# Feed-forward of a decoder layer: on VectorE the third h value moves ahead of the two roundings, and the next tile's first h value ahead of the second maximum

## The chip, the cores and the metric

The kernel runs on one core of one Trainium2 chip. The metric is the device time of one execution in microseconds (us). The engines are named as the profile names them: PE is TensorE's matmuls, PEld its weight loads, DVE is VectorE, ACT is ScalarE, POOL is GpSimd, SP is SyncE.

## The reference, cut to what matters

A decoder layer over 4 x 512 = 2048 tokens of 512 values: windowed attention, a routed expert layer, and a quantized feed-forward. The change lies in the feed-forward alone:

```python
def bit_linear(x, w):           # both sides rounded: x to 8 bits per token, w to -1, 0, 1
    return einsum('bsh,oh->bso', activation_quant(x), weight_quant(w))
def activation_quant(x):
    s = 127 / clip(max(abs(x), axis=-1), 1e-5)
    return clip(round(x * s), -128, 127) / s
h = silu(bit_linear(x, w_gate)) * bit_linear(x, w_up)     # 512 -> 2048
h = ln_weight * (h * rsqrt(mean(h * h) + 1e-6))
y = bit_linear(h, w_down)                                  # 2048 -> 512
x = x + y                                                  # x was layer-normed first
```

So each token needs the mean square and the largest weighted absolute value over all 2048 of its h values before the first of them can be rounded.

## The kernel before, in words

There is no scheduler: each engine has a program written out by hand, and runs its instructions in that order. Semaphores between the engines are waited for by the instruction in front, so everything behind it on that engine waits too.

The feed-forward goes over 16 tiles of 128 tokens (`TILES`), and each tile's 2048 h values are made in four chunks c = 0 to 3 of 512 columns (`FC`, `CHK`). A name such as h2 below means chunk 2 of h. Around one chunk stand these steps:

- PE, `gate_up(t, c)`: four matmuls for the gate sums and four for the up sums, in two pairs of PSUM buffers in turn. It may write pair c % 2 again once the h value two chunks back exists. The profile calls the four buffers `e_xT_ps`, `up_ps`, `e_z_ps` and `e_aT_ps`, since the expert phase used the same space.
- ACT, `gate_of(t, c)`: silu of the gate sums into `f_gate` (L1746).
- DVE, `hidden(t, c)`: h = up sums x scale x gate (L1784), one input from PSUM and one from SBUF. It counts up `h_ready`.
- POOL, `weighted(t, c)`: h times the norm's weight, into `hw`, which the profile calls `xg_own` (L1695), 128x512 in SBUF from two SBUF inputs.

Once per tile, one tile late (for t - 1 while tile t's chunks are made), come: on DVE `top_of(t-1, 0)` and `top_of(t-1, 1)`, the largest absolute value of each half of `hw` (L1800, `hw_max`); on ACT `squares` (L1754), sums of squares by halves; on DVE `sum_squares(t-1)` (L1805, L1807); on POOL `rms_of(t-1)`, a power of -1/2 (L1691, `h_rms`); on DVE `scale_h(t-1)` (L1813 to L1822), five operations on one column that end in `h_mul`; on DVE `quantize_h(t-1)`, the two roundings (L1831, `hq_big`), each 128x1024 floats from SBUF to SBUF, called hq0 and hq1 below; on ACT `pack(t-1, 0)` and `pack(t-1, 1)` (L1739, `hq`), which narrow the codes, in order after `gate_of(t, 2)` and ahead of `gate_of(t, 3)`. SP transposes the halves by DMA, and PE multiplies them into the output two tiles late (`down`, L1906), a quarter behind each `gate_up`. DVE adds the output to x (`y_of`, L1836), and POOL scatters it and fetches a later tile (`store`, `gather`).

Between these stand the front steps for the layer norm and rounding of the x of later tiles: `mean_of`, `top_of_x` (L1191), `scale_x`, `quantize_x` (L1206, `xq_big`, 128x512 from SBUF to SBUF), `stats_of` and `variance_of` on DVE.

POOL's order within tile t is: `rms_of(t-1)`, `weighted(t, 0)`, `weighted(t, 1)`, `weighted(t, 2)`, `rstd_of`, `weighted(t, 3)`, `gu_scale_of`, `store`, `gather`. The four products are called w0 to w3 below.

Of the kernel before, what the change touches and what calls it, by code (L numbers as in the profile page):

```python
# [1579 lines left out]
def ffn_phase(nc, ctx, io, x2, y, sh, front):  # L1580
# [59 lines left out]
    def inside(t):  # L1640
        return 0 <= t < TILES

    def flat(tile, i):
        return tile[:, i].rearrange("p c n -> p (c n)")
# [17 lines left out]
    def sums_of(t):  # L1662
        return gate_ps[0][:] if t == TILES - 1 else up_ps[0][:] if t == TILES - 2 else y_ps[:]
# [115 lines left out]
    def vector_program(dve):  # L1779
        def hidden(t, c):  # L1780
            i = t % 2
            dve.wait_ge(gate_ready, t * FC + c + 1)
            dve.wait_ge(up_summed, t * FC + c + 1)
            nc.vector.scalar_tensor_tensor(h[:, i, c, :], up_ps[c % 2][:], gu_scale[:, i, 1:2], gate[:, c % 2, :],  # L1784
                                           ALU.mult, ALU.mult).then_inc(h_ready, 1)

        def weighted_last():
            t, c = TILES - 1, FC - 1
            dve.wait_ge(h_ready, TILES * FC)
            nc.vector.tensor_tensor(hw[:, t % 2, c, :], h[:, t % 2, c, :], ln_w[:, c * CHK:c * CHK + CHK], ALU.mult)\  # L1790
                .then_inc(hw_last_ready, 1)

        def top_of(t, n):
            i = t % 2
            if (t, n) == (TILES - 1, HALVES - 1):
                dve.wait_ge(hw_ready, TILES * FC - 1)
                dve.wait_ge(hw_last_ready, 1)
            else:
                dve.wait_ge(hw_ready, t * FC + 2 * n + 2)
            nc.vector.tensor_reduce(hw_max[:, i, n:n + 1], flat(hw, i)[:, n * HALF:n * HALF + HALF], AX.X, ALU.max,  # L1800
                                    apply_absolute_value=True).then_inc(hw_max_ready, 1)

        def sum_squares(t):
            dve.wait_ge(sq_ready, (t + 1) * HALVES)
            nc.vector.tensor_reduce(h_ss[:], h_sq[:, t % 2, :], AX.X, ALU.add).then_inc(ss_ready, 1)  # L1805
            dve.wait_ge(ss_ready, t + 1)
            nc.vector.tensor_scalar(h_var[:], h_ss[:], 1.0 / F, RMS_EPS, ALU.mult, ALU.add).then_inc(h_var_ready, 1)  # L1807

        def scale_h(t):
            i = t % 2  # L1810
            at = t * HQ_STEPS
            dve.wait_ge(hw_max_ready, (t + 1) * HALVES)
            nc.vector.tensor_reduce(h_top[:], hw_max[:, i, :], AX.X, ALU.max).then_inc(hq_step, 1)  # L1813
            dve.wait_ge(hq_step, at + 1)
            dve.wait_ge(rms_ready, t + 1)
            nc.vector.tensor_scalar(h_max[:], h_top[:], h_rms[:], Q_EPS, ALU.mult, ALU.max).then_inc(hq_step, 1)
            dve.wait_ge(hq_step, at + 2)
            nc.vector.reciprocal(h_inv[:], h_max[:]).then_inc(hq_step, 1)
            nc.vector.tensor_scalar(y_scale[:, t % (LATE_DOWN + 2):t % (LATE_DOWN + 2) + 1], h_max[:], w_mean[:, 2:3], 1.0 / QMAX, ALU.mult, ALU.mult)\
                .then_inc(hq_step, 1)  # L1820
            dve.wait_ge(hq_step, at + 4)
            nc.vector.tensor_scalar(h_mul[:], h_inv[:], h_rms[:], QMAX, ALU.mult, ALU.mult).then_inc(hq_step, 1)  # L1822

        def quantize_h(t):
            i = t % 2
            dve.wait_ge(hq_step, (t + 1) * HQ_STEPS)
            for n in range(HALVES):
                cols = slice(n * HALF, n * HALF + HALF)
                if inside(t - 1):
                    dve.wait_ge(hq_packed, (t - 1) * HALVES + n + 1)  # L1830
                nc.vector.tensor_scalar(hq_big[:, cols], flat(hw, i)[:, cols], h_mul[:], CODE, ALU.mult, ALU.add)\  # L1831
                    .then_inc(hq_ready, 1)

        def y_of(t):
            dve.wait_ge(y_summed, t + 1)
            nc.vector.scalar_tensor_tensor(xt[t], sums_of(t), y_scale[:, t % (LATE_DOWN + 2):t % (LATE_DOWN + 2) + 1], xt[t],  # L1836
                                           ALU.mult, ALU.add).then_inc(y_ready, 1)

        for t in range(TILES):
            if inside(t + 2):  # L1840
                front.mean_of(dve, t + 2)
            if inside(t - 1):
                top_of(t - 1, 0)
            if inside(t - LATE_DOWN - 1):
                y_of(t - LATE_DOWN - 1)
            if inside(t - 1):
                top_of(t - 1, 1)
            hidden(t, 0)
            if t == 0:
                dve.wait_ge(front.product_ready, ROUTED_TILES)  # L1850
                nc.vector.tensor_tensor(xg[last_expert], y_ps[:], xg[last_expert], ALU.add).then_inc(front.x2_ready, 1)
            if inside(t - 1):
                sum_squares(t - 1)
            if inside(t + 2):
                front.top_of_x(dve, t + 2)
            hidden(t, 1)
            if inside(t + 2):
                front.scale_x(dve, t + 2)
            if inside(t - 1):
                scale_h(t - 1)  # L1860
                quantize_h(t - 1)
            hidden(t, 2)
            if inside(t + 2):
                front.quantize_x(dve, t + 2)
            if inside(t + 3):
                front.stats_of(dve, t + 3)
                front.variance_of(dve, t + 3)
            if t == TILES - 1:
                top_of(t, 0)
            hidden(t, 3)  # L1870
        last = TILES - 1
        weighted_last()
        top_of(last, 1)
        sum_squares(last)
        scale_h(last)
        quantize_h(last)
        y_of(last - LATE_DOWN)
        for t in range(TILES - LATE_DOWN, TILES):
            y_of(t)

    def tensor_program(pe):
# [43 lines left out]
        for g in range(FC):  # L1925
            if g + 1 < FC:
                transpose_h(last, g + 1)
            down(last, g)

    return sync_program, gpsimd_program, scalar_program, vector_program, tensor_program  # L1930


# [93 lines left out]
```

## Time and profile before

| | us |
|---|---|
| median of 3 executions (788.45 to 791.21) | 789.06 |
| the profiled execution, its own time | 788.65 |
| its span | 786.6 |
| DVE busy in the span | 592.7 (75%) |
| PE busy in the span | 734.1 (93%) |
| POOL busy in the span | 331.8 (42%) |
| granted clock of PE, mean of the span | 0.989 |

The span is the time from the first to the last instruction of the profiled execution; the 2.05 us beside it are outside the program. Shares of the whole span mix three phases: attention up to about 455 us, the experts up to about 590 us, the feed-forward behind that. Times in rows of the trace count from the span's start.

### The profile page before, as it was taken

To read this page: it belongs to the slowest core of one execution; us is meant where nothing else is said; L and a number is where in the kernel's file an instruction comes from. 1 tells how busy PE (TensorE), PEld (TensorE's weight loads), DVE (VectorE), ACT (ScalarE), POOL (GpSimd) and SP (SyncE) were. 2 spreads that over 40 slices of the span, in tenths; PEclk is the share of its full clock that TensorE was granted. 3 is DMA by queue.
4 is the path that set the end of the run, shared out by engine and by line. 5 is a ranking of instruction groups with operands and counts; after the bars stand their busy time and mean duration, and the time that the engine had idled before them with its cause. 6 is when DMAs were issued, how large, how long until landed. Compare 5 with 4: busy or idle time off the path is not lost.

```text
span 786.6 us, 14189 instructions
## 1 busy us (share of the span) xinstructions
PE 734.1 (93%) x5167; PEld 509.8 (65%) x5184; DVE 592.7 (75%) x1099; ACT 473.0 (60%) x1028; POOL 331.8 (42%) x329
## 2 busy tenths in 40 slices
PE   5988999999999999999987989999998999999993
PEld 4765777777777776777764678888874444444441
DVE  6886866886667866766666547888888999999992
ACT  4565666766676665766666314444456777667761
POOL 2011205213242134254554444445546577778661
PEclk9999999999999999999999999999999999999998
DMA  9300012304030321314301366555341133334241
GB/s 311 119 1 27 28 47 89 105 31 162 29 108 28 108 93 70 108 38 152 129 34 55 54 216 261 186 200 196 118 134 30 41 95 80 98 91 107 70 92 40
DMA packets 55474, 78.33 MB, mean 100 GB/s; under 512 B 36335, under 2 KB 38383, under 8 KB 53680
## 3 DMA queue, kind: packets, MB, share of 16 engines
q1 hardware_dynamic: 46336, 51.99, 20.8%
q0 software_dynamic: 8784, 24.93, 9.7%
q8 instruction: 43, 0.70, 0.4%
q10 hardware_dynamic: 288, 0.52, 0.2%
q14 instruction: 23, 0.19, 0.1%
HBM read 56.92 MB, written 17.59 MB: 95 GB/s over the span
## 4 chain that ended last, share of the span: by engine, by line
PE 61%; DVE 21%; issue 7%; ACT 5%; POOL 3%; DMA 1%; another core or an unknown queue 0%; SPq 0%; ACTq 0%; POOLq 0%; DVEq 0%
PE side_ps L889 17%; PE pT_ps L976 9%; PE e_z_ps L1528 7%; PE y_ps L1528 7%; PE s_ps L948 5%; PE pv_ps L998 5%; DVE h L1784 4%; DVE hw_max L1800 4%; DVE hq_big L1831 3%; ACT hq L1739 2%; DVE neg_max L724 2%; PE s_ps L956 2%; PE pT_ps L889 1%; DVE probs L745 1%; ACT probs L548 1%
## 5 line engine op out<-in xcount | busy, mean ns | idle before, releaser
L548 ACT ACTIVATE probs<-s_ps,neg_max 128x512 f32<-128x512 f32 (+2 forms) x256 | 152.3, 610 | 18.6 <-DVE neg_max L724 17.1
L724 DVE TENSOR_REDUCE neg_max<-s_ps 128x2 f32<-128x1024 f32 (+2 forms) x128 | 124.5, 1014 | 36.2 <-PE s_ps L956 35.1
L976 PE MATMUL pT_ps<-ident,probs 128*128 128x128 f32 x832 | 115.7, 281 | 8.7 <-DVE probs L745 8.0
L560 ACT ACTIVATE probs<-pT_ps 128x512 f32<-128x512 f32 x96 | 57.4, 598 | 97.0 <-PE pT_ps L976 96.2
L976 PEld LDWEIGHTS pT_ps<-ident,probs 128*128 128x128 f32 x832 | 94.3, 144 | 23.9 <-DVE probs L745 10.6
L745 DVE COPY probs<-pT_ps 128x512 f32<-128x512 f32 x112 | 76.7, 685 | 38.9 <-PE pT_ps L976 35.9
L1695 POOL TENSOR_TENSOR xg_own<-h,ln_w_sb 128x512 f32<-128x512 f32 x63 | 82.8, 1324 | 33.2 <-DVE h L1784 33.1
L889 PE MATMUL side_ps<-w_hi 128*128 128x512 f32 x172 | 71.0, 413 | 0.0
L412 POOL TENSOR_TENSOR aT_hi<-norm,one_col 128x512 fp32r<-128x512 f32 x15 | 15.6, 1042 | 124.6 <-DVE norm L736 86.3
L889 PE MATMUL side_ps<-w_hi,w_lo 128*128 128x512 f32 x172 | 67.4, 392 | 0.0
L889 PE MATMUL side_ps<-w_lo,w_hi 128*128 128x512 f32 x172 | 67.0, 390 | 0.0
L1906 PE MATMUL y_ps<-w_tern,hqT 128*128 128x512 bf16 x210 | 54.5, 379 | 0.7
L998 PE MATMUL pv_ps<-probs,v_sb 128*32 128x256 f32 (+1 forms) x896 | 52.4, 368 | 1.9 <-DVE probs L745 0.9
L404 POOL TENSOR_TENSOR norm<-rinv,one_col 128x512 f32<-128x512 f32 x16 | 16.7, 1041 | 86.8 <-DVE rinv L731 86.8
L548 ACT ACTIVATION_READ_ACCUMULATOR probs<-s_ps,neg_max 128x1 f32 x256 | 52.9, 207 | 0.0
L1739 ACT ACTIVATE hq<-hq_big,minus_offset 128x1024 bf16<-128x1024 f16 x30 | 33.0, 1142 | 30.4 <-DVE hq_big L1831 30.4
L1657 PE MATMUL e_xT_ps<-w_tern,xqT_home 128*128 128x512 bf16 x126 | 32.7, 380 | 7.1 <-DVE h L1784 6.2
L1800 DVE TENSOR_REDUCE hw_max<-xg_own 128x1 f32<-128x1024 f32 x32 | 38.7, 1209 | 0.3
L998 PEld LDWEIGHTS pv_ps<-probs,v_sb 128*32 128x32 f32 x896 | 25.0, 109 | 19.6 <-issue 6.7
L889 PEld LDWEIGHTS side_ps<-w_hi,w_lo 128*128 128x128 f32 x172 | 32.3, 188 | 7.4
L1906 PEld LDWEIGHTS y_ps<-w_tern,hqT 128*128 128x128 bf16 x224 | 21.4, 98 | 23.3
L889 PEld LDWEIGHTS side_ps<-w_hi 128*128 128x128 f32 x172 | 32.4, 188 | 5.8 <-DVE k_lo L648 0.5
(290 smaller groups left out, 1782.8 us busy)
## 6 DMA issues: line engine op xcount, KB each, us to landing
w_piece<-w_ffn SPq DMA_DIRECT2D x24, 512.0 KB
w_stage<-w_ffn SPq DMA_DIRECT2D x12, 1024.0 KB
xres<-x POOLq DMA_DIRECT2D x4, 1024.0 KB, 6.4
xn<-x SPq DMA_DIRECT2D x3, 1024.0 KB
x<-xres POOLq DMA_DIRECT2D x3, 1024.0 KB, 4.8
xn<-c SPq DMA_DIRECT2D x2, 1024.0 KB, 5.0
v_next<-c SPq DMA_DIRECT2D x2, 1024.0 KB, 7.3
xn<-x SPq DMA_DIRECT2D x4, 256.0 KB, 3.7
```

Source lines behind the costliest of these rows:

```text
L548: nc.scalar.activation(weights[qt][:, h, at:at + width(qt)], s_ps[:, h, 0:width(qt)], ACT.Exp, bias=neg_max[:, qt % 2, h:h + 1], accum_out ...
L560: nc.scalar.activation(out, turned_p, ACT.Identity).then_inc(slot_copied[0], 1)
L724: nc.vector.tensor_reduce(neg_max[:, qt % 2, 2 * s:2 * s + 2], s_ps[:, 2 * s:2 * s + 2, 0:width(qt)], AX.X, ALU.max, negate=True).then_inc ...
L745: nc.vector.tensor_copy(weights[qt][:, :, a:z], pT_ps[:, 1, :].rearrange("p (h n) -> p h n", h=GH))\
L889: last = nc.tensor.matmul(out, lt, r, start=(first and n == 0), stop=(final and n == len(terms) - 1))
L976: last = nc.tensor.transpose(pT_ps[:, k % 2, h * P:h * P + P], weights[qt][:, h, a:z], ident[:])
L998: last = nc.tensor.matmul(pv_ps[HD * h:HD * h + HD, to], v_sb[:, slot, f:f + HD], p, start=first, stop=final, tile_position=(0, HD * h))
L1528: last = nc.tensor.matmul(out, lt[:, k, :], r[:, at, :], start=(n == 0), stop=(n == 3 * DK - 1))
L1695: nc.gpsimd.tensor_tensor(hw[:, t % 2, c, :], h[:, t % 2, c, :], ln_w[:, c * CHK:c * CHK + CHK], ALU.mult)\
L1739: nc.scalar.activation(hq[:, cols], hq_code[:, cols], ACT.Identity, bias=minus_offset[:]).then_inc(hq_packed, 1)
L1800: nc.vector.tensor_reduce(hw_max[:, i, n:n + 1], flat(hw, i)[:, n * HALF:n * HALF + HALF], AX.X, ALU.max, apply_absolute_value=True).then_ ...
L1906: last = nc.tensor.matmul(sums_of(t), hqT[:, t % 2, k, :], down_w[:, k, :], start=(k == 0), stop=(k == FK - 1))
```

## The change

Within one tile of the DVE program, two steps change places with a neighbour. The instructions, their shapes, their buffers and their waits stay as they are, and so do the programs of the other engines.

```diff
             if inside(t - LATE_DOWN - 1):
                 y_of(t - LATE_DOWN - 1)
-            if inside(t - 1):
-                top_of(t - 1, 1)
             hidden(t, 0)
...
             if inside(t - 1):
                 sum_squares(t - 1)
+                top_of(t - 1, 1)
             if inside(t + 2):
                 front.top_of_x(dve, t + 2)
             hidden(t, 1)
...
             if inside(t - 1):
                 scale_h(t - 1)
+            hidden(t, 2)
+            if inside(t - 1):
                 quantize_h(t - 1)
-            hidden(t, 2)
             if inside(t + 2):
                 front.quantize_x(dve, t + 2)
```

The first place is on DVE at the start of a tile in the middle of the feed-forward (`h<-up_ps` is h0 here, `hw_max` the maxima, `xn<-y_ps` the output's addition). Before:

```order
L1800 TENSOR_REDUCE hw_max<-xg_own 128x1
L1836 SCALAR_TENSOR_TENSOR xn<-y_ps,y_scale,xn 128x512
L1800 TENSOR_REDUCE hw_max<-xg_own 128x1
L1784 SCALAR_TENSOR_TENSOR h<-up_ps,gu_scale,f_gate 128x512
L1805 TENSOR_REDUCE h_ss<-h_sq 128x1
L1807 TENSOR_SCALAR h_var<-h_ss 128x1
L1191 TENSOR_REDUCE x_max<-f_xn 128x1
```

And of the change, the same stretch:

```order
L1836 SCALAR_TENSOR_TENSOR xn<-y_ps,y_scale,xn 128x512
L1784 SCALAR_TENSOR_TENSOR h<-up_ps,gu_scale,f_gate 128x512
L1805 TENSOR_REDUCE h_ss<-h_sq 128x1
L1807 TENSOR_SCALAR h_var<-h_ss 128x1
L1800 TENSOR_REDUCE hw_max<-xg_own 128x1
L1191 TENSOR_REDUCE x_max<-f_xn 128x1
```

The second maximum has moved behind h0, `h_ss` and `h_var`, and stands in front of `x_max`.

The second place is later in the same tile on DVE, around the two roundings (`h<-up_ps` is h2 here, `hq_big` x2 are hq0 and hq1). Before:

```order
L1819 TENSOR_SCALAR y_scale<-h_max,w_mean 128x1
L1822 TENSOR_SCALAR h_mul<-h_inv,h_rms 128x1
L1831 TENSOR_SCALAR hq_big<-xg_own,h_mul 128x1024 x2
L1784 SCALAR_TENSOR_TENSOR h<-up_ps,gu_scale,f_gate 128x512
L1206 TENSOR_SCALAR xq_big<-f_xn,x_inv 128x512
```

And of the change:

```order
L1819 TENSOR_SCALAR y_scale<-h_max,w_mean 128x1
L1822 TENSOR_SCALAR h_mul<-h_inv,h_rms 128x1
L1784 SCALAR_TENSOR_TENSOR h<-up_ps,gu_scale,f_gate 128x512
L1831 TENSOR_SCALAR hq_big<-xg_own,h_mul 128x1024 x2
L1206 TENSOR_SCALAR xq_big<-f_xn,x_inv 128x512
```

h2 now stands between `h_mul` and the roundings.

## Rows read from the trace of the kernel before

**Rows 1.** The profile's page: the chain that ended last, by engine.

```profile
PE 61%; DVE 21%; issue 7%; ACT 5%; POOL 3%; DMA 1%; another core or an unknown queue 0%; SPq 0%; ACTq 0%; POOLq 0%; DVEq 0%
```

**Rows 2.** Busy time by engine in a stretch: tiles 0 to 13 of the feed-forward.

```profile
core 0: us, PE busy (x) PEld busy (x) DVE busy (x) ACT busy (x) POOL busy (x), PEclk, DMA share, GB/s
592.60:743.20 150.60, 143.41 (x675) 62.98 (x686) 142.88 (x318) 107.67 (x162) 107.01 (x113) 1.00 0.29 75
```

**Rows 3.** DVE in order of time: h3 of tiles 0, 13 and 14.

```profile
598.26 0.75 DVE L1784 SCALAR_TENSOR_TENSOR h<-e_aT_ps,gu_scale,f_gate 128x512 f32<-128x512 f32 x1
...
743.17 0.75 DVE L1784 SCALAR_TENSOR_TENSOR h<-e_aT_ps,gu_scale,f_gate 128x512 f32<-128x512 f32 x1 [1.11 <-ACT f_gate L1746]
...
753.67 0.75 DVE L1784 SCALAR_TENSOR_TENSOR h<-e_aT_ps,gu_scale,f_gate 128x512 f32<-128x512 f32 x1 [1.13 <-ACT f_gate L1746]
```

**Rows 4.** DVE in order of time, from h3 of tile 8 to h3 of tile 9.

```profile
687.05 0.75 DVE L1784 SCALAR_TENSOR_TENSOR h<-e_aT_ps,gu_scale,f_gate 128x512 f32<-128x512 f32 x1
687.72 0.20 DVE L1186 TENSOR_SCALAR mean_rstd<-f_bn_mv,f_rstd 128x1 f32<-128x1 f32 x1
687.84 1.21 DVE L1800 TENSOR_REDUCE hw_max<-xg_own 128x1 f32<-128x1024 f32 x1
...
689.63 1.21 DVE L1800 TENSOR_REDUCE hw_max<-xg_own 128x1 f32<-128x1024 f32 x1
690.75 0.74 DVE L1784 SCALAR_TENSOR_TENSOR h<-up_ps,gu_scale,f_gate 128x512 f32<-128x512 f32 x1
...
691.59 0.15 DVE L1807 TENSOR_SCALAR h_var<-h_ss 128x1 f32<-128x1 f32 x1
...
692.26 0.74 DVE L1784 SCALAR_TENSOR_TENSOR h<-e_aT_ps,gu_scale,f_gate 128x512 f32<-128x512 f32 x1
...
693.90 0.21 DVE L1822 TENSOR_SCALAR h_mul<-h_inv,h_rms 128x1 f32<-128x1 f32 x1
694.15 1.30 DVE L1831 TENSOR_SCALAR hq_big<-xg_own,h_mul 128x1024 f32<-128x1024 f32 x1
695.37 0.74 DVE L1831 TENSOR_SCALAR hq_big<-xg_own,h_mul 128x1024 f32<-128x1024 f32 x1
696.03 0.73 DVE L1784 SCALAR_TENSOR_TENSOR h<-up_ps,gu_scale,f_gate 128x512 f32<-128x512 f32 x1
696.69 0.47 DVE L1206 TENSOR_SCALAR xq_big<-f_xn,x_inv 128x512 f32<-128x512 f32 x1
...
698.28 0.75 DVE L1784 SCALAR_TENSOR_TENSOR h<-e_aT_ps,gu_scale,f_gate 128x512 f32<-128x512 f32 x1
```

**Rows 5.** POOL in the same tile: w3 of tile 8, then w0, w1, w2.

```profile
687.88 1.27 POOL L1695 TENSOR_TENSOR xg_own<-h,ln_w_sb 128x512 f32<-128x512 f32 x1 [0.29 <-DVE h L1784]
...
692.40 2.49 POOL L1695 TENSOR_TENSOR xg_own<-h,ln_w_sb 128x512 f32<-128x512 f32 x2
...
696.85 1.45 POOL L1695 TENSOR_TENSOR xg_own<-h,ln_w_sb 128x512 f32<-128x512 f32 x1 [1.96 <-DVE h L1784]
```

**Rows 6.** ACT in the same tile: the gate of h0, then the two packs.

```profile
689.21 0.67 ACT L1746 ACTIVATE f_gate<-e_xT_ps,gu_scale 128x512 f32<-128x512 f32 x1
...
695.48 1.15 ACT L1739 ACTIVATE hq<-hq_big,minus_offset 128x1024 bf16<-128x1024 f16 x1 [2.17 <-DVE hq_big L1831]
...
696.54 1.13 ACT L1739 ACTIVATE hq<-hq_big,minus_offset 128x1024 bf16<-128x1024 f16 x1
```

**Rows 7.** Tile 14: DVE's roundings hq0, hq1 and POOL's w0, w1.

```profile
749.31 0.88 DVE L1831 TENSOR_SCALAR hq_big<-xg_own,h_mul 128x1024 f32<-128x1024 f32 x1
...
750.11 1.76 DVE L1831 TENSOR_SCALAR hq_big<-xg_own,h_mul 128x1024 f32<-128x1024 f32 x1
...
748.38 1.26 POOL L1695 TENSOR_TENSOR xg_own<-h,ln_w_sb 128x512 f32<-128x512 f32 x1
...
749.61 1.72 POOL L1695 TENSOR_TENSOR xg_own<-h,ln_w_sb 128x512 f32<-128x512 f32 x1
```

**Rows 8.** The last tile's first rounding, with POOL doing nothing.

```profile
768.76 0.75 DVE L1831 TENSOR_SCALAR hq_big<-xg_own,h_mul 128x1024 f32<-128x1024 f32 x1
```

**Rows 9.** PE's waits in tiles 0 to 13: waited for, us in total, times, longest.

```profile
PE e_xT_ps L1657 <- DVE h L1784: 6.1, 14, 1.7
```

## The prediction

> **What bounds the kernel now.** The chain that ended last, on the page, gives PE 61% and DVE 21% [rows 1], but it mixes three phases. So the next view is the busy time by stretches. In the first fourteen tiles of the feed-forward PE is busy 143.4 of 150.6 us, DVE 142.9, ACT and POOL some 107 each [rows 2]. Two engines at 95% do not say which of them holds the other, nor whether a third does. For that I read one tile in order of time, with h3 of tile 8 at 687.05 as zero; the pattern repeats with h3 of tile 9 at 698.28 [rows 4], so a tile is 11.23 us. The mean from tile 0 to tile 13 is (743.17 - 598.26) / 13 = 11.15 us [rows 3].
>
> I follow h3 of tile 9 back. It starts 1.74 us after the second pack, and the second pack 1.06 after the first, at 9.49 and 8.43 [rows 6]. The first pack starts 0.03 after hq0 ends (694.15 + 1.30 = 695.45, or 8.40). Why does hq0 take 1.30 us? Undisturbed it takes 0.75 [rows 8]. POOL's w0 and w1 run back to back from 692.40 to 694.89 [rows 5], and hq0 ends 0.56 after that: it stood still until w1 was done. Tile 14 repeats it with w0: w0 ends at 748.38 + 1.26 = 749.64, hq0 at 749.31 + 0.88 = 750.19, again 0.55 later [rows 7]. So a rounding and a POOL product do not run at the same time. h2, h1 and the maxima take their usual 0.74 and 1.21 us beside POOL [rows 4].
>
> The loop is thus: h3, 0.83 later w3 on POOL (687.88), POOL's row of work up to the end of w1 at 7.84, hq0's rest of 0.56, the two packs, the last gate, h3 at 11.23. DVE has hardly any slack beside it (it is busy almost throughout), and PE is held a little behind: in these tiles it waits 14 times for h, 6.1 us in total [rows 9].
>
> **The change part by part.** Nothing is added or removed; four instructions are reordered per tile. I lay out one tile again, zero at h3.
>
> *h0 ahead of the second maximum.* That maximum started at 2.58 [rows 4]; h0 could start there. But its gate ends on ACT at 689.21 + 0.67 = 689.88, or 2.83 [rows 6], so h0 starts at 2.85, and DVE stands for 0.27. ACT's order up to this gate hangs on h3 (the squares of h2 and h3), which doesn't change. From here distances are those of [rows 4]. h0 to `h_var` is 0.84: 3.69. `h_var` to h1 is 0.67, and the maximum put between adds the 1.12 that it took before (689.63 to 690.75): h1 at 5.48, against 5.21 before. So this half alone makes DVE 0.27 later, since its stand for the gate is new. h1 to `h_mul` is 1.64: 7.12. What else `scale_h` needs is there: POOL's w0 starts at 5.35 [rows 5], behind `h_rms`. Of the second maximum nothing else is waiting. Earlier h0 helps PE, whose wait for it goes away, and POOL not at all: POOL is busy with `store` and `gather` until `h_rms`.
>
> *h2 ahead of the roundings.* h2 doesn't need `h_mul`, so it follows it after 0.12 (as the first maximum follows the equally short `mean_rstd`) to 0.25 (as hq0 does) [rows 4]; I take 0.13, since nothing is waited for: h2 at 7.25. hq0 follows h2 after 0.66, as `xq_big` does: 7.91. w1 ends at 7.84, so hq0 is free of it and takes 0.75 [rows 8]: it ends at 8.66. That is 0.26 later than before, although the standstill is gone: h2 took its time.
>
> Now the point of the sum: h2 releases w2 on POOL. w2 started 0.82 after h2 (696.03 to 696.85) and took 1.45 instead of 1.27 [rows 4, 5]: `xq_big` had started 0.66 after h2 and it stood behind that one. In the new order hq0 stands exactly where `xq_big` stood, 0.15 ahead of w2. So hq0 comes first, and w2 is waiting at 8.07 when hq1 starts at 7.91 + 0.67 = 8.58. Tile 14 shows that situation [rows 7]: w1 waiting since 749.61 behind hq0, hq1 started at 750.11. There POOL went in between: w1 ended at 751.33, which is 1.13 after hq0's end, and hq1 at 751.87, 0.55 after that, so it took 1.76. The same here: w2 ends at 9.79, hq1 at 10.34 (before: 9.06). The second pack starts at 10.34 + 0.04 = 10.38 in place of 9.49, and h3 1.74 later: 12.12.
>
> A tile then lasts 12.12 us in place of 11.23, that is +0.89. Of this, 0.63 is hq1 late behind w2, 0.26 hq0 late. Does the loop close? POOL's row from h3 to the end of w1 is unchanged at 7.84, and w2, done at 9.79, is ahead of `rstd_of` and w3. DVE has over a microsecond to spare, so nothing on it is late. PE has about 10.8 us of work in a tile and waits the rest for h3.
>
> A rule of the Trainium skill bears on this. SBUF — State Buffer, section on who interferes with whom, says that VectorE in its two-port modes and GpSimd exclude each other, that whichever issues first has the pair of ports for its whole instruction, and that the other fully blocks. The order by issue agrees with the rows. Read to the letter, each would wait the other's whole duration: w2 ends at 8.66 + 1.27 = 9.93, hq1 at 10.68, h3 at 12.46, a tile 0.34 longer than by the rows. The rows of tile 14 (1.13 and 0.55 in place of 1.27 and 0.75) decide, and I take theirs.
>
> *Sum.* Thirteen tiles from tile 0's h3 to tile 13's took 144.91 us [rows 3]. Thirteen of 12.12 are 157.56: +12.65. Tile 1 may be up to 0.3 shorter, since in tile 0 no rounding came before. Tile 14 took 10.50 (743.17 to 753.67): it has no x steps and its hq1 is already held by w1, but the second pack still stands ahead of h3, and w2 now takes w1's place; between 0 and +0.9, I take +0.8, since hq0 again comes after h2. In tile 15 the last gate stands ahead of the second pack, so hq1 doesn't hold h3: 0 to +0.1. Behind it nothing changes. Together 12.65 + 0.8 - 0.25 = +13.2. Against the profiled execution's own 788.65 that is 801.85; the median is 0.41 above it, so I say 802.2. Its own range is 800 to 805 (tile 1 and 14 by their ends, 0.12 per tile for the start of h2, and rounding of rows over 13 tiles).
>
> **The rivals.**
>
> *A, the rule to the letter.* 13 x 0.34 = 4.4 more: 806.6. For it the rule, against it two measured ends in tile 14. 4%.
>
> *B, DVE keeps the ports from hq0 to hq1.* hq1 starts only 0.08 before hq0 ends; if w2 were not let in, hq1 would end at 9.33, the second pack would start when the first lets it (8.70 + 1.06 = 9.76), and h3 at 11.50: +0.27 per tile, +3.5, or 792.6. Against it tile 14, where POOL was let in. 5%.
>
> *C, w2 first.* The lead of hq0 is 0.15 us. If POOL won it, w2 would end at 8.07 + 1.27 = 9.34, hq0 at 9.89, hq1 at 10.56; the second pack follows the first, 9.93 + 1.06 = 10.99, h3 at 12.73: +1.50 per tile, 808 to 809. Against it `xq_big`, which won with the same lead. 4%.
>
> *D, faster.* PE is the bound in truth, and the loop through POOL has slack that the rows hide. Then h0 earlier by 0.85 takes away PE's wait in front of the third chunk, some 0.3 in a usual tile (6.1 us in 14 waits, with a long one of 1.7 [rows 9]): 13 x 0.3 = -3.9, or 785.2. It decides only where the second pack can start by 9.19; even with hq1 in time it needs hq0's end at 8.10, and hq0 would have to start at 7.35, when `h_mul` is just written. Against it stands, too, that PE's waits are for h and not the other way. 5%.
>
> *E, no change.* Some slack in the packs that I don't see takes up the delay: 787 to 791. The last gate starts straight behind the second pack in each tile, so there is hardly room. 4%.
>
> **How the numbers follow.** My forecast has 78%. With A it makes 82%, and both lie in 797 to 807; below that I leave room for a gate or a pack that turns out a quarter of a microsecond shorter per tile. B, C, D and E are left out. About 0.3% (2.4 us) is what a measurement of this kernel can tell from no change. Slower by more than that are the forecast, A, B and C: 91%. Within it E, 4%; faster D, 5%.
>
> **What the changed profile would show.** hq0 in usual tiles about 0.75 us in place of 1.30; hq1 about 1.76 in place of 0.74; w2 about 1.7 us, started 0.8 behind h2 with no wait on POOL ahead of it; the second pack preceded by a wait on ACT of some 0.6 for `hq_big`; h0 waiting for its gate by 0.25 to 0.3; h3 to h3 at 12.1; PE's wait for h now in front of the second chunk, for h3, over a microsecond each. I am wrong if hq1 stays at 0.75 (B), if hq0 takes about 1.9 (C), or if the tile stays near 11.2 although hq1 is late. One thing could come on top: PE's granted clock is 1.00 in this stretch [rows 2], the 2.4 GHz level, and with PE standing over 1 us in each tile it might fall to 1.2 GHz in places; nothing of this stretch shows that it does.

## The result, and the profile after

The change made the kernel slower, about as much as forecast.

| | before | after |
|---|---|---|
| median, us | 788.75 (787.71 to 791.21, 4 runs) | 802.43 (801.09 to 805.49, 4 runs) |
| ratio to before | | 1.0172, 95% interval 1.0151 to 1.0194 |
| span of the profiled execution, us | 786.6 | 800.2 |
| DVE busy in the span, us | 592.7 | 598.6 |
| h3 of tile 0 to h3 of tile 15, us | 165.89 | 179.36 |
| behind h3 of tile 15, us | 22.5 | 22.5 |

The ratio is +13.6 us, within +11.9 to +15.3. The fifteen stretches between the h3 rows of tiles 0 and 15 took 13.5 us longer together, and what lies ahead of them and behind them took as long as before (598.41 us in place of 598.26, and 22.5), so the whole loss lies between the h3 rows. I read the same tile as in [rows 4], again with h3 of tile 8 (695.22) as zero. First DVE in order of time (start, duration, engine, line, operation; the bracket is idle time and what ended it):

```profile
598.41 0.75 DVE L1784 SCALAR_TENSOR_TENSOR h<-e_aT_ps,gu_scale,f_gate 128x512 f32<-128x512 f32 x1
...
695.22 0.75 DVE L1784 SCALAR_TENSOR_TENSOR h<-e_aT_ps,gu_scale,f_gate 128x512 f32<-128x512 f32 x1 [0.39 <-ACT f_gate L1746]
...
698.08 0.75 DVE L1784 SCALAR_TENSOR_TENSOR h<-up_ps,gu_scale,f_gate 128x512 f32<-128x512 f32 x1 [0.20 <-ACT f_gate L1746]
698.74 0.14 DVE L1805 TENSOR_REDUCE h_ss<-h_sq 128x1 f32<-128x2 f32 x1
698.92 0.15 DVE L1807 TENSOR_SCALAR h_var<-h_ss 128x1 f32<-128x1 f32 x1
699.00 1.21 DVE L1800 TENSOR_REDUCE hw_max<-xg_own 128x1 f32<-128x1024 f32 x1
...
700.71 0.74 DVE L1784 SCALAR_TENSOR_TENSOR h<-e_aT_ps,gu_scale,f_gate 128x512 f32<-128x512 f32 x1
...
702.36 0.21 DVE L1822 TENSOR_SCALAR h_mul<-h_inv,h_rms 128x1 f32<-128x1 f32 x1
702.49 0.74 DVE L1784 SCALAR_TENSOR_TENSOR h<-up_ps,gu_scale,f_gate 128x512 f32<-128x512 f32 x1
703.15 0.74 DVE L1831 TENSOR_SCALAR hq_big<-xg_own,h_mul 128x1024 f32<-128x1024 f32 x1
703.81 1.77 DVE L1831 TENSOR_SCALAR hq_big<-xg_own,h_mul 128x1024 f32<-128x1024 f32 x1
705.50 0.47 DVE L1206 TENSOR_SCALAR xq_big<-f_xn,x_inv 128x512 f32<-128x512 f32 x1
...
707.37 0.75 DVE L1784 SCALAR_TENSOR_TENSOR h<-e_aT_ps,gu_scale,f_gate 128x512 f32<-128x512 f32 x1 [0.39 <-ACT f_gate L1746]
...
777.77 0.74 DVE L1784 SCALAR_TENSOR_TENSOR h<-e_aT_ps,gu_scale,f_gate 128x512 f32<-128x512 f32 x1
```

hq0 and hq1 have changed places as the long one: 1.30 and 0.74 us before [rows 4], 0.74 and 1.77 now. Beside them POOL in the same stretch, w0 with w1, w2, and w3 of tile 9:

```profile
700.57 2.49 POOL L1695 TENSOR_TENSOR xg_own<-h,ln_w_sb 128x512 f32<-128x512 f32 x2
703.31 1.72 POOL L1695 TENSOR_TENSOR xg_own<-h,ln_w_sb 128x512 f32<-128x512 f32 x1 [0.25 <-DVE h L1784]
...
708.20 1.28 POOL L1695 TENSOR_TENSOR xg_own<-h,ln_w_sb 128x512 f32<-128x512 f32 x1 [0.59 <-DVE h L1784]
```

w2 starts 0.16 us after hq0, ends at 703.31 + 1.72 = 705.03, that is 1.14 us behind hq0's end (703.89), and hq1 ends 0.55 us behind w2 (705.58). In [rows 5] w2 lay behind both roundings. ACT then shows whom the late hq1 holds up: the second pack, and behind it the gate of h3.

```profile
703.93 1.15 ACT L1739 ACTIVATE hq<-hq_big,minus_offset 128x1024 bf16<-128x1024 f16 x1 [3.28 <-DVE hq_big L1831]
705.61 1.15 ACT L1739 ACTIVATE hq<-hq_big,minus_offset 128x1024 bf16<-128x1024 f16 x1 [0.54 <-DVE hq_big L1831]
706.67 0.67 ACT L1746 ACTIVATE f_gate<-e_z_ps,gu_scale 128x512 f32<-128x512 f32 x1
```

Between the packs ACT now stands for 0.54 us; in [rows 6] the second followed the first at once. What PE waits for in tiles 0 to 12 (total, times, longest), and its busy time there, close the picture:

```profile
PE e_z_ps L1657 <- DVE h L1784: 16.7, 12, 2.9
```

```profile
core 0: us, PE busy (x) PEld busy (x) DVE busy (x) ACT busy (x) POOL busy (x), PEclk, DMA share, GB/s
592.80:746.60 153.80, 135.98 (x640) 59.24 (x652) 141.21 (x300) 103.67 (x155) 105.54 (x109) 0.99 0.27 71
```

PE's wait has moved from the third chunk's buffers (`e_xT_ps`, [rows 9]) to the second chunk's, which need h3, 1.4 us each on average with one of 2.9. PE is held up here, not holding. Its granted clock is 0.99 in this stretch against 1.00 before. All of the difference lies in tile 2, right behind that longest wait:

```profile
611.05 1.89 PE L1657 MATMUL e_z_ps<-w_tern,xqT_home 128*128 128x512 bf16 x4 [2.91 <-DVE h L1784]
```

From there seven matmuls took some 0.63 us each in place of 0.38, and the granted clock of 612 to 614 us is 0.53: the 1.2 GHz level for about 3 us. The tile lasted 12.14 us like its neighbours, so it cost nothing here.

The end behind h3 of tile 15 is as long as before, but not for want of a change. First PE there before, from the first matmul of tile 14's output, then after:

```profile
764.73 3.63 PE L1906 MATMUL up_ps<-w_tern,hqT 128*128 128x512 bf16 x16 [0.40 <-DMA hqT<-hq]
769.57 0.62 PE L1889 MATMUL hT_ps<-f_ident,hq_big 128*128 128x128 f16 x8 [1.21 <-DVE hq_big L1831]
```

```profile
779.48 3.63 PE L1906 MATMUL up_ps<-w_tern,hqT 128*128 128x512 bf16 x16 [2.39 <-DMA hqT<-hq]
783.19 0.62 PE L1889 MATMUL hT_ps<-f_ident,hq_big 128*128 128x128 f16 x8
```

The transposes of tile 14 reach PE 1.1 us later, seen from h3 of tile 15 (1.71 us behind it in place of 0.58). PE had stood 1.21 us for the last tile's first rounding, and this wait took the delay up: both kernels start `hT_ps` 5.42 us behind h3.

### The profile page after: what moved, and what is told of

Same layout as the page of the kernel before. It is cut to its first block, busy times and chain, and to the rows that moved or that the text cites. A ratio compares the mean times of both kernels' runs of the same rounds, so it can differ in the third digit from the quotient of the medians.

```text
span 800.2 us, 14189 instructions
## 1 busy us (share of the span) xinstructions
PE 733.8 (92%) x5167; PEld 507.9 (63%) x5184; DVE 598.6 (75%) x1099; ACT 474.8 (59%) x1028; POOL 336.3 (42%) x329
## 4 chain that ended last, share of the span: by engine, by line
PE 60%; DVE 20%; issue 10%; ACT 6%; POOL 2%; DMA 0%; another core or an unknown queue 0%; ACTq 0%; SPq 0%; DVEq 0%; POOLq 0%
PE side_ps L889 17%; PE pT_ps L976 9%; PE e_z_ps L1528 7%; PE y_ps L1528 7%; PE pv_ps L998 5%; PE s_ps L948 5%; DVE hq_big L1831 5%; DVE h L1784 3%; DVE neg_max L724 3%; ACT sq_junk L1754 2%; ACT f_gate L1746 2%; PE s_ps L956 2%; DVE probs L745 2%; PE pT_ps L889 1%; DVE hw_max L1800 1%
## 5 line engine op out<-in xcount | busy, mean ns | idle before, releaser
L976 PE MATMUL pT_ps<-ident,probs 128*128 128x128 f32 x832 | 114.0, 277 | 10.5 <-DVE probs L745 9.2
L976 PEld LDWEIGHTS pT_ps<-ident,probs 128*128 128x128 f32 x832 | 92.6, 142 | 25.7 <-DVE probs L745 11.9
L1695 POOL TENSOR_TENSOR xg_own<-h,ln_w_sb 128x512 f32<-128x512 f32 x63 | 86.3, 1376 | 21.6 <-DVE h L1784 21.5
L1657 PE MATMUL e_z_ps<-w_tern,xqT_home 128*128 128x512 bf16 x128 | 34.0, 389 | 18.5 <-DVE h L1784 18.5
L1831 DVE TENSOR_SCALAR hq_big<-xg_own,h_mul 128x1024 f32<-128x1024 f32 x32 | 37.8, 1223 | 0.0
```

Source lines behind the costliest of these rows:

```text
L976: last = nc.tensor.transpose(pT_ps[:, k % 2, h * P:h * P + P], weights[qt][:, h, a:z], ident[:])
L1695: nc.gpsimd.tensor_tensor(hw[:, t % 2, c, :], h[:, t % 2, c, :], ln_w[:, c * CHK:c * CHK + CHK], ALU.mult)\
```

## The experiments

Every kernel was timed against the kernel before on its own chip, whose medians there were 786.6 to 786.7 us. Ratios are therefore what to compare. Beside them stands what one profiled execution shows: h3 of tile 0 to h3 of tile 15, and what lies behind that, as differences to before (165.89 and 22.46 us).

| kernel | usual tile, us | h3 to h3 | behind | sum | measured, from the ratio |
|---|---|---|---|---|---|
| before | 11.23 | | | | |
| the change | 12.14 | +13.5 | 0.0 | +13.5 | +13.6 (11.9 to 15.3) |
| h0 half alone | 11.24, 10.97 | -1.2 | +0.1 | -1.2 | -0.4 (-1.5 to +0.7) |
| h2 half alone | 11.86 | +10.7 | +1.4 | +12.1 | +12.0 (9.7 to 14.2) |
| change, w2 waits | 11.50 | +3.6 | +1.0 | +4.5 | +4.1 (2.7 to 5.5) |
| h2 half, w2 waits | 11.24 | +1.1 | +1.2 | +2.3 | +2.0 (0.7 to 3.2) |
| change, gate first | 11.57 | +5.6 | 0.0 | +5.6 | +7.2 (5.5 to 9.0) |
| h2 between the roundings | 12.11 | +10.2 | 0.0 | +10.2 | +11.0 (9.1 to 12.8) |
| h0 half, gate first | 11.04, 10.97 | -2.7 | +0.2 | -2.5 | -2.2 (-3.2 to -1.3) |
| change, w2 waits, gate first | 11.50 | +3.6 | +1.2 | +4.8 | +5.0 (3.1 to 6.8) |
| h2 half, w2 waits, gate first | 10.58 | -8.2 | +1.2 | -7.0 | -5.6 (-7.0 to -4.2) |
| the same, tile 15 as before | 10.58 | -7.8 | 0.0 | -7.8 | -8.3 (-10.9 to -5.6) |

A usual tile is one from 5 to 11, which have a gather on POOL; where two numbers stand, the second is a tile without (2 to 4).

**Which half costs?** The two halves apart. The first keeps only this edit:

```diff
-            if inside(t - 1):
-                top_of(t - 1, 1)
             hidden(t, 0)
...
                 sum_squares(t - 1)
+                top_of(t - 1, 1)
```

Expected: 

> Only the first half of the change: h0 and the sum of squares ahead of the second maximum, the roundings in front of h2 as before. Theory (GpSimd's product w2 gets in between the two roundings once h2 stands ahead of them): here w2 stays behind both roundings, so hq0 still stands still until w1 is done (about 1.3 us), hq1 takes 0.74. Where GpSimd has a gather before h_rms the tile stays near 11.2; where it has none, h_rms and with it w1 come earlier and the tile falls to about 10.9. In all 0 to -2.5 us against the kernel before, about -1.3 (787.4). Rival (each half costs by itself, since h1 and h_mul come 0.27 later on VectorE): +0.27 in 13 tiles, +3.5 us.

Measured: ratio 0.9995 (0.9981 to 1.0009), no difference. By the rows it saves 1.2 us, in tiles 3, 4 and 13 to 15; hq0 took 1.0 us in tiles 5 to 12, where POOL has a gather ahead of w0 and w1, and 0.75 in tiles 1 to 4 and 13, where it has none. The time cannot tell -1.2 from nothing, but it excludes the rival's +3.5, which the h0 half would have cost by itself.

The second half alone:

```diff
                 scale_h(t - 1)
+            hidden(t, 2)
+            if inside(t - 1):
                 quantize_h(t - 1)
-            hidden(t, 2)
```

Expected: 

> Only the second half: h2 ahead of the two roundings, the two maxima as before. Theory: the loss is here. hq1 about 1.76 us, w2 about 1.71, a tile about 11.85, in all about +10 us (798.8). Rival (the two halves are needed together, or the first half carries most): under +5 us.

Measured: 1.0152 (1.0123 to 1.0181). hq1 took 1.75 to 1.77 us and w2 1.71, the tile 11.86. The loss is here. The end behind h3 of tile 15 grew by 1.4 us, which I had not expected. In this profiled execution that is PE's clock:

```profile
774.67 5.31 PE L1907 MATMUL up_ps<-w_tern,hqT 128*128 128x512 bf16 x16 [2.08 <-DMA hqT<-hq]
```

PE stood 2.08 us, and then the sixteen matmuls that take 3.63 us in the kernel before and in the changed one took 5.31; the granted clock of 776 to 778 us is 0.50, the 1.2 GHz level. The transposes themselves were no later than in the changed kernel, whose end didn't grow. Whether the other executions of this kernel had the same drop isn't known.

**Is it w2?** The whole change with one wait on POOL, so that w2 can't come in between:

```diff
             weighted(t, 0)
             weighted(t, 1)
+            if inside(t - 1):
+                pool.wait_ge(hq_ready, t * HALVES)
             weighted(t, 2)
```

Expected: 

> The whole change, and GpSimd waits with w2 until hq1 is done. Nothing else differs. Theory: hq0 and hq1 both 0.75 us, w2 1.27; the second pack starts when the first lets it; a tile about 11.5 us, in all +4 us against the kernel before (792.8), that is 9 us under the changed kernel, although a wait was added. Rival (hq1 is long for another reason than w2, such as its place behind h2): hq1 stays over 1.5 us and the time stays at 802 or more, since w2 is only made later.

Measured: 1.0052 (1.0034 to 1.0070), 790.49 us. The roundings of all tiles, as this kernel's trace groups them (duration in ns, min/median/max), and then w2 with its new wait:

```profile
L1833 DVE TENSOR_SCALAR hq_big<-xg_own,h_mul x32: 743/746/753, 603.2 to 770.9; 128x1024 f32<-128x1024 f32 x32
```

```profile
696.64 1.45 POOL L1695 TENSOR_TENSOR xg_own<-h,ln_w_sb 128x512 f32<-128x512 f32 x1 [1.57 <-DVE hq_big L1833]
```

In the changed kernel the same group reads 743/750/1771. A wait added on POOL takes 9 to 10 us off the change, and no rounding is long any more: w2 between the roundings is shown as the cause of that part. What is left, +0.27 a tile, is the other part, hq0 being later. The same wait with the h2 half alone:

Expected: 

> Only the second half (h2 ahead of the roundings), with w2 waiting for hq1. Theory: hq0 starts when w1 is about done and takes 0.75 to 0.85, hq1 0.74; what h2 costs in front of hq0 is what hq0 stood still for before, so the tile stays at 11.2; in all 0 to +1.5 us (about 789.7). Rival (h2 in front of the roundings costs its own 0.66 us in each tile): +8 us or more.

Measured: 1.0025 (1.0009 to 1.0041). The tile is 11.24, as before: h2 ahead of hq0 costs nothing, since hq0 (0.76 to 0.78 us here) had stood still for as long. The +2 us lie in tile 2 (11.55 against 10.74), tile 14 (11.08 against 10.50) and 1.2 behind h3 of tile 15, less 0.4 in tile 15. In tile 2 a stretch at the 1.2 GHz level has a part (granted clock 0.50 from 611 to 613 us): tile 3 is back at 11.21.

**Does it act through the second pack?** On ACT the last gate ahead of it, first with the whole change:

```diff
-            if inside(t - 1) and t < TILES - 1:
-                pack(t - 1, 1)
             gate_of(t, 3)
-            if t == TILES - 1:
+            if inside(t - 1):
                 pack(t - 1, 1)
```

Expected: 

> The whole change, and on ScalarE the last gate of a tile stands ahead of the second pack (as it does in tile 15 already). Theory: hq1 is as late as in the changed kernel (1.76 us, behind w2), but h3 no longer waits for it; the tile is then held by VectorE's own order with the long hq1 in it, about 11.6 us, in all +5.3 us against the kernel before. Rival (the delay of h3 comes from VectorE's order alone and not by way of the second pack): the tile stays at 12.1 and the time at +13.

Measured: 1.0092 (1.0070 to 1.0115). hq1 is as long as ever (1.76), but the tile fell from 12.14 to 11.57. So the delay reached h3 by way of the pack. What holds the tile now is DVE's own order: from 620 to 740 us DVE waits for nothing. The time, +7.2 us, is above the +5.3 expected, which lies outside the interval (5.5 to 9.0); the trace shows +5.6, at its edge.

**Who gets in, and does it hold for another instruction?** h2 between the two roundings:

```diff
                 scale_h(t - 1)
-                quantize_h(t - 1)
+                quantize_h(t - 1, (0,))
             hidden(t, 2)
+            if inside(t - 1):
+                quantize_h(t - 1, (1,))
```

Expected: 

> Not the change, but h2 between the two roundings: hq0, h2, hq1; maxima as before. hq1 now starts 0.66 us after h2 and w2 0.82, so by the order of asking hq1 wins and takes 0.75, w2 comes between hq1 and xq_big, and xq_big stands still behind w2. Theory: hq1 0.75, w2 about 1.7, xq_big about 1.5 in place of 0.47 us, a tile about 12.2, in all +11 us. Rival (only hq_big suffers, because it is twice as long; or VectorE keeps the ports over instructions that follow each other): xq_big stays at 0.47, tile 11.5, +3.6 us.

Measured: 1.0140 (1.0116 to 1.0163), tile 12.11. DVE in tile 8 of this kernel, from hq0 to `xq_big`, and POOL's w2:

```profile
688.70 1.27 DVE L1831 TENSOR_SCALAR hq_big<-xg_own,h_mul 128x1024 f32<-128x1024 f32 x1
689.89 0.74 DVE L1784 SCALAR_TENSOR_TENSOR h<-up_ps,gu_scale,f_gate 128x512 f32<-128x512 f32 x1
690.55 0.74 DVE L1831 TENSOR_SCALAR hq_big<-xg_own,h_mul 128x1024 f32<-128x1024 f32 x1
691.21 1.49 DVE L1206 TENSOR_SCALAR xq_big<-f_xn,x_inv 128x512 f32<-128x512 f32 x1
...
690.71 1.71 POOL L1695 TENSOR_TENSOR xg_own<-h,ln_w_sb 128x512 f32<-128x512 f32 x1 [1.29 <-DVE h L1784]
```

hq1 started 0.16 ahead of w2 and took its 0.74. w2 was waiting when `xq_big` started, and now that one, 0.47 us at best, takes 1.49. In these rows the order is that of asking, with any of the three; DVE doesn't keep its turn from one instruction to the next.

**Is there a version that beats both?** The loop of the forecast runs through the second pack and through hq0 tied to w1. To cut it in both places takes the h2 half, the wait for w2 and the last gate first:

Expected: 

> The second half alone (h2 ahead of the roundings), w2 waits for hq1, and the last gate stands ahead of the second pack. Theory: with all three the loop through the second pack is cut and no rounding stands still for long; the tile falls to 10.6 to 10.9 us, which is PE's own work. Thirteen tiles give -4 to -5 us, of which up to 1.2 us is lost at the end, where PE waits for the transposes of tile 14 as it did in the run with w2 waiting: -2.7 to -4.2 us in all. Rival (the loop is closed elsewhere, in GpSimd's row of gather and products): tile stays at 11.2, time within 1 us of before.

Measured: 0.9929 (0.9911 to 0.9947), 781.25 us. The tile is 10.58, and the time -5.6 us (-7.0 to -4.2), both better than expected. Against the run with the h2 half and w2 waiting, the gate edit alone took the tile from 11.24 to 10.58. Neither this edit by itself on the kernel before nor the three without the wait for w2 was run. The same gate edit on the h0 half:

Expected: 

> The first half alone (h0 ahead of the second maximum), with the last gate ahead of the second pack. Theory: hq0 is still tied to w1 and w1 to GpSimd's gather, so tiles with a gather stay at 11.1 and those without fall to 10.9; about -2 us in all. Rival (the pack was what held the tile): tiles of 10.8 throughout, -5 us.

Measured: 0.9972 (0.9959 to 0.9984), 784.45 us: small gain, tied to the gather as expected.

With all helps in place, what does the h0 half cost?

Expected: 

> The whole change with w2 waiting for hq1 and the last gate ahead of the second pack, so that against the run with only the second half and the same two helps, the one difference is h0 ahead of the second maximum. Theory: the first half's own price is on VectorE (h0 stands for its gate, then h1, h_mul, h2 and the roundings come later), and it shows in full once nothing else holds the tile: a tile of about 11.5 us in place of 10.6, in all +4 us against the kernel before (791). Rival (the first half costs nothing once GpSimd is out of the way): 10.6 us, -5 us.

Measured: 1.0063 (1.0040 to 1.0086). The tile is 11.50 in place of 10.58. That is the h0 half's price beside the h2 half, 0.92 us a tile, hidden in the earlier runs under other holds. The expectation put it down to DVE's order. The trace shows more: DVE is busy 10.30 us of the tile and stands for h0's gate. First ACT up to that gate, then h0:

```profile
697.42 1.15 ACT L1741 ACTIVATE hq<-hq_big,minus_offset 128x1024 bf16<-128x1024 f16 x1 [3.28 <-DVE hq_big L1831]
698.47 0.67 ACT L1748 ACTIVATE f_gate<-e_z_ps,gu_scale 128x512 f32<-128x512 f32 x1
699.04 1.14 ACT L1741 ACTIVATE hq<-hq_big,minus_offset 128x1024 bf16<-128x1024 f16 x1
...
702.37 0.67 ACT L1748 ACTIVATE f_gate<-e_xT_ps,gu_scale 128x512 f32<-128x512 f32 x1
```

```profile
703.07 0.75 DVE L1784 SCALAR_TENSOR_TENSOR h<-up_ps,gu_scale,f_gate 128x512 f32<-128x512 f32 x1 [0.96 <-ACT f_gate L1748]
```

This is a second loop: hq0, first pack, last gate, second pack, the two squares, the gate of h0, h0, and 5.07 us of DVE work from h0 to the next hq0, with h2 in it. Gate and second pack both stand in it, whichever comes first, so the gate edit leaves the 11.50 of the run before unchanged. With the h0 half alone, where the roundings stand ahead of h2, DVE takes 4.53 us from h0 to hq0, and the tiles without a gather last 10.97, with the gate edit and without: 0.53 less in both. In the kernel before, with the second maximum ahead of h0, it is 3.39 us, and DVE waits for no gate in a usual tile.

The kernel with 781.25 us still lost 1.2 us at its end. PE's waits there, from 736 us to the end:

```profile
PE up_ps L1907 <- DMA hqT<-hq: 2.4, 2, 1.6
PE e_xT_ps L1907 <- ACT hqT L1733: 0.8, 1, 0.8
```

PE waits for the transposed halves of tile 14 and starts the last tile's own transposes only behind that. So tile 15 alone goes back to the old order:

```diff
+            if t == TILES - 1:
+                quantize_h(t - 1)
             hidden(t, 2)
-            if inside(t - 1):
+            if inside(t - 1) and t < TILES - 1:
                 quantize_h(t - 1)
```

Expected: 

> As the run with the second half, w2 waiting and the last gate ahead of the second pack (781.3), but tile 15 keeps the old order (both roundings ahead of h2, no wait for w2), because there PE waited for the transposes of tile 14 and passed this on to the last tile's transposes. Theory: the end behind h3 of tile 15 is 22.5 us again in place of 23.7, tiles 0 to 14 as they were; in all -6 to -7 us against the kernel before (780). Rival (what tile 15 gets back at its end it loses ahead of h3, the alternation of roundings and products being slower): same as 781.3.

Measured: 0.9895 (0.9861 to 0.9929), 778.87 us, the fastest version of the study: 8 us under the kernel before. Tile 15 took 0.4 us more than with h2 ahead of its roundings and the end 1.2 less, so the rival was right in part. First PE's wait for the transposes over the whole feed-forward, 0.4 us again, then the middle of the feed-forward by busy times:

```profile
PE up_ps L1909 <- DMA hqT<-hq: 0.4, 1, 0.4
```

```profile
core 0: us, PE busy (x) PEld busy (x) DVE busy (x) ACT busy (x) POOL busy (x), PEclk, DMA share, GB/s
609.00:736.00 127.00, 125.87 (x618) 57.54 (x619) 122.59 (x286) 97.09 (x145) 95.22 (x102) 1.00 0.33 88
```

PE is busy 99% of that stretch. Before it was 95% in [rows 2], and 97% from 619.75 to 743.17 us, which leaves out the first tiles as this one does. To go on from here PE's work itself would have to shrink, and DVE's with it: DVE is busy 122.59 of the same 127 us.

## Why the prediction was right, point by point

The zero is h3 of tile 8 in all of this; the first number is the forecast's.

- **The loop that held a tile before** (POOL's products, hq0 tied to w1, packs, last gate): confirmed by cutting it. With the last gate ahead of the second pack, h2 in the place of hq0's standstill and w2 out of the way, the tile fell to 10.58, and with the h0 half alone it is 10.97 in place of 11.24 where no gather delays w1.
- **h0 starts at its gate, not where the maximum stood:** 2.85 against 2.86, with ACT's gate named as what ended the wait.
- **h1, h_mul, h2, hq0:** 5.48, 7.12, 7.25, 7.91 against 5.49, 7.14, 7.27, 7.93. The assumed 0.12 to 0.25 from `h_mul` to h2 was 0.13.
- **hq0 free, 0.75 us:** 0.74.
- **w2 between the roundings:** ends at 9.79 against 9.81; hq1 ends at 10.34 against 10.36, after 1.77 us. Shown as the cause by the run in which w2 waits.
- **Second pack at 10.38, h3 at 12.12:** 10.39 and 12.15, and by the mean of the usual tiles 12.14.
- **The ends:** tile 1 took 11.83 (forecast up to 0.3 under 12.12), tile 14 11.29 (+0.8, as taken), tile 15 10.56 (at most +0.1).
- **Behind h3 of tile 15, "nothing changes":** right in the time, 22.5 us both times, and by luck. PE's wait for the transposes of tile 14 grew from 0.40 to 2.39 us, and the last tile's first rounding left just enough room for it.
- **The sum:** +13.2 against 13.5 by the rows. The 0.3 left over is the 0.02 a tile.

Of the rivals, the rule to the letter (A) fell: w2 ended 1.14 behind hq0 and hq1 0.55 behind w2, not 1.27 and 0.75. DVE keeping its turn (B) and w2 first (C) fell with hq1's 1.77 and hq0's 0.74. PE as the true bound (D) fell for the change; it became true only with 10.58, when all else was out of the way. That also shows the "about 10.8 us" of PE work in a tile as too much by 0.2: the same matmuls fitted into 10.58.

Some smaller statements were off. I wrote that POOL would start w2 with no wait ahead of it; it stood 0.25 us for h2, as my own times had it (w1 done at 7.84, w2 at 8.07). h0 waited for its gate 0.20 us as the view counts it, not 0.25 to 0.3. DVE was to have over a microsecond to spare; it is busy 11.32 of the 12.15 us, which leaves 0.83. PE's clock did fall to the lower level, in tile 2, without cost there. And I split the +0.89 of a tile into 0.63 for w2 and 0.26 for the order on DVE. As differences with other things fixed this holds (12.14 to 11.50 with w2 waiting, 11.50 to 11.23 the rest). But the prediction closes the changed tile by POOL's row to w1, and hq0 no longer hangs on w1 (done at 7.84, hq0 at 7.93). The path that it follows itself, from h3 by the squares and h0's gate to h0, is the loop now, and with no other hold the h0 half costs 0.92 a tile beside the h2 half.

## What to carry to other kernels

Where instructions of VectorE and GpSimd exclude each other, as the rounding and the product do here, a reordering on one changes whose turn comes next on the other: ask which instruction of the other engine the moved step releases, and whether it will be waiting when yours starts. A rounding that stands still is no loss if the standstill is off the loop; look at what follows, here two packs and a gate. And price each half of a change with the other holds taken away: the h0 half measured as nothing by itself, and cost 0.92 us a tile beside the h2 half once the other holds were gone. An instruction that moves up to where it waits for another engine ties the two together: ask what that engine does ahead of it.

## What was unexpected

- A GpSimd product that stands behind a VectorE rounding ends 1.12 to 1.14 us after it, against 1.26 to 1.28 alone, and a rounding behind a product 0.55 to 0.56 after, against 0.75 alone (up to 0.61 where only the product's last 0.2 us stood against it). So standing costs less than the other's remaining time plus one's own duration. [rows 7] had it already, and it held in every kernel where the two met.
- A lead of 0.15 to 0.18 us was enough to be first in every tile where it arose (hq0 in the changed kernel and with the h2 half alone, hq1 with h2 between, `xq_big` before).
- The whole gain of 8 us came by adding a wait and changing two orders, with no work taken out.
- The end of the kernel before has 1.2 us of room and no more. In the changed kernel the second pack of tile 14 starts 1.0 us ahead of h3 of tile 15 in place of 1.7, and the end is as before. In the four kernels in which w2 waits for the roundings in tile 15 too, it starts only 0.1 us ahead, and through the two transposes by DMA, behind which PE starts the last tile's own, the end is 1.0 to 1.25 us longer.
